# Splitting the first load of A by row tile in a three-term float32 matrix kernel

## The reference

```python
base = x @ W.T                                   # W: 1024 x 1024
gates1 = top-2 softmax of (x @ Wr.T + 5 * one_hot(language))      # 8 experts
c = base + 2 * sum over experts of gates1[e] * (x @ A[e].T) @ B[e].T   # rank 16
y = c @ Wf.T + bf
gates2 = softmax(c @ Wrf.T)                      # 4 experts
y = y + 2 * sum over experts of gates2[e] * (c @ Af[e].T) @ Bm[e].T    # rank 8
out = x + y
```

## Time and profile before

| | |
|---|---|
| device time, median of 3 runs | 324.57 us (324.01 to 324.74) |
| the profiled execution's own time | 324.45 us |
| its span in the trace | 323.1 us |
| PE busy | 319.5 us, 99% |
| DVE busy | 245.1 us, 76% |
| ACT busy | 127.9 us, 40% |
| HBM read and written | 18.97 MB and 8.39 MB |

### The profile page before, as it was taken

One profiled execution on the slowest core, in us unless ns is written; L12 is line 12 of the kernel. 1 busy time (PEld: TensorE's weight loads), 2 busy tenths in 40 slices (PEclk: granted clock), 3 DMA queues, 4 the chain that ended last, 5 costly groups with the idle time before them and its releaser, 6 DMA issues.

```text
span 323.1 us, 5951 instructions
## 1 busy us (share of the span) xinstructions
PE 319.5 (99%) x2255; PEld 313.4 (97%) x2255; DVE 245.1 (76%) x540; ACT 127.9 (40%) x253; POOL 1.4 (0%) x11
## 2 busy tenths in 40 slices
PE   8999999999999999999999999999999999999996
PEld 5999999999999899899999999999999999999996
DVE  3999999998799778988866856757585595665543
ACT  3882846495147236225413503411430340342111
POOL 1000000000000000000000000000000000000000
PEclk9999999999999999999999999999999999999999
DMA  7999000000000311700330250060042015003003
GB/s 261 416 408 284 9 2 0 2 0 2 0 2 0 132 30 40 262 0 0 115 149 0 73 187 0 14 245 0 0 144 116 0 65 195 0 0 130 0 0 130
DMA packets 10702, 27.55 MB, mean 85 GB/s; under 512 B 3166, under 2 KB 4702, under 8 KB 10688
## 3 DMA queue, kind: packets, MB, share of 16 engines
q1 hardware_dynamic: 10256, 26.83, 23.5%
q10 hardware_dynamic: 432, 0.53, 0.5%
HBM read 18.97 MB, written 8.39 MB: 85 GB/s over the span
## 4 chain that ended last, share of the span: by engine, by line
PE 98%; DMA 1%; DVE 0%; issue 0%
PE sums L1269 97%; DMA in<-part 1%; PE sums L1508 1%; DVE rows L1047 0%; DVE b_high L775 0%
## 5 line engine op out<-in xcount | busy, mean ns | idle before, releaser
L1269 PE MATMUL sums<-b_high,a_high 128*128 128x256 f32 (+1 forms) x224 | 45.9, 289 | 0.2 <-DVE b_high L775 0.2
L1269 PE MATMUL sums<-b_low,a_high 128*128 128x256 f32 (+1 forms) x224 | 45.5, 287 | 0.0
L1269 PE MATMUL sums<-b_high,a_low 128*128 128x256 f32 (+1 forms) x224 | 45.5, 286 | 0.0
L1269 PEld LDWEIGHTS sums<-b_high,a_high 128*128 128x128 f32 x224 | 35.2, 191 | 1.1 <-ACT a_high L527 1.1
L1269 PEld LDWEIGHTS sums<-b_low,a_high 128*128 128x128 f32 x224 | 35.1, 191 | 0.0
L1269 PEld LDWEIGHTS sums<-b_high,a_low 128*128 128x128 f32 x224 | 34.9, 190 | 0.0
L1047 DVE TENSOR_TENSOR rows<-sums,rows 128x354 f32<-128x354 f32 x48 | 24.4, 522 | 9.7 <-PE sums L1269 9.3
L1047 DVE TENSOR_TENSOR narrow<-sums,narrow 128x244 f32<-128x244 f32 x30 | 12.4, 412 | 25.6 <-PE sums L1269 25.6
L1269 PE MATMUL sums<-t_high,s_high 128*128 128x354 f32 x96 | 31.6, 329 | 0.0
L1269 PE MATMUL sums<-t_low,s_high 128*128 128x354 f32 x96 | 31.1, 324 | 0.0
L1269 PE MATMUL sums<-t_high,s_low 128*128 128x354 f32 x96 | 31.1, 324 | 0.0
(11 more groups left out here) (149 smaller groups left out, 821.9 us busy)
## 6 DMA issues: line engine op xcount, KB each, us to landing
stage<-tokens SPq DMA_DIRECT2D x14, 512.0 KB, 4.1
out<-rows SPq DMA_DIRECT2D x14, 512.0 KB, 4.8
in<-part SPq DMA_DIRECT2D x7, 585.0 KB, 9.0
in<-part SPq DMA_DIRECT2D x4, 777.0 KB, 14.1
in<-part SPq DMA_DIRECT2D x4, 265.0 KB, 16.6
rows<-tokens SPq DMA_DIRECT2D x2, 512.0 KB, 14.1
out<-rows SPq DMA_DIRECT2D x3, 192.0 KB, 2.3
c_plain<-gate_proj SPq DMA_DIRECT2D x1, 544.0 KB, 18.3
```

What stands on the lines that cost most here:

```text
L1269: return nc.tensor.matmul(out_, lhs, rhs, start=start, stop=stop, skip_group_check=True)
```

## The change

A's columns for row tiles 0 and 1 come in two transfers of 128 columns instead of one of 256. ACT rounds each in an instruction of its own, DVE subtracts each in an instruction of its own, and PE's first six matmuls stand in another order. The number and the shapes of the matmuls are as before. One transfer is added on SP's queue ahead of everything else that SP issues.

```diff
-        here_2_first = [sem(f"here_2_first_{i}") for i in range(3)]
+        here_2_first = [sem(f"here_2_first_{i}") for i in range(4)]
...
-            sp.dma_start(in_2[:, 0, 2 * P:ROWS_A], part_2[0, :, 2 * P:ROWS_A]).then_inc(here_2_first[0], 16)
+            sp.dma_start(in_2[:, 0, row_tile(0)], part_2[0, :, row_tile(0)]).then_inc(here_2_first[0], 16)
+            sp.dma_start(in_2[:, 0, row_tile(1)], part_2[0, :, row_tile(1)]).then_inc(here_2_first[3], 16)
             sp.dma_start(in_2[:, 0, 0:2 * P], part_2[0, :, 0:2 * P]).then_inc(here_2[0], 16)
...
             act.wait_ge(here_2_first[0], 16)
-            copy(a_high[:, 0, 2 * P:ROWS_A], a12[:, 0, 2 * P:ROWS_A]).then_inc(first_high, 1)
+            copy(a_high[:, 0, row_tile(0)], a12[:, 0, row_tile(0)]).then_inc(first_high, 1)
+            act.wait_ge(here_2_first[3], 16)
+            copy(a_high[:, 0, row_tile(1)], a12[:, 0, row_tile(1)]).then_inc(first_high, 1)
...
             dve.wait_ge(first_high, 1)
-            low_part(a_low[:, 0, 2 * P:ROWS_A], a12[:, 0, 2 * P:ROWS_A], a_high[:, 0, 2 * P:ROWS_A])\
-                .then_inc(first_low, 1)
+            low_part(a_low[:, 0, row_tile(0)], a12[:, 0, row_tile(0)], a_high[:, 0, row_tile(0)]).then_inc(first_low, 1)
             dve.wait_ge(first_b_high, 1)
             low_part(b_low[:, 0, 0:CUT[1]], b21[:, 0, 0:CUT[1]], b_high[:, 0, 0:CUT[1]]).then_inc(first_low, 1)
             dve.wait_ge(first_high, 2)
+            low_part(a_low[:, 0, row_tile(1)], a12[:, 0, row_tile(1)], a_high[:, 0, row_tile(1)]).then_inc(first_low, 1)
+            dve.wait_ge(first_high, 3)
             low_part(a_low[:, 0, 0:2 * P], a12[:, 0, 0:2 * P], a_high[:, 0, 0:2 * P]).then_inc(first_low, 1)
...
             pe.wait_ge(first_high, 1)
             pe.wait_ge(first_b_high, 1)
-            for dt in range(2):
-                rows_product(0, dt, 0, HH)
+            rows_product(0, 0, 0, HH)
             pe.wait_ge(first_low, 1)
-            for dt in range(2):
-                rows_product(0, dt, 0, LH)
+            rows_product(0, 0, 0, LH)
+            pe.wait_ge(first_high, 2)
+            rows_product(0, 1, 0, HH)
             pe.wait_ge(first_low, 2)
             for dt in range(2):
                 rows_product(0, dt, 0, HL)
             pe.wait_ge(first_low, 3)
+            rows_product(0, 1, 0, LH)
+            pe.wait_ge(first_low, 4)
             tiles_product(0, 1, 0)
```

More of the change, by code:

```diff
@@ L781, in vector_program @@
             dve.wait_ge(first_high, 2)
+            low_part(a_low[:, 0, row_tile(1)], a12[:, 0, row_tile(1)], a_high[:, 0, row_tile(1)]).then_inc(first_low, 1)
+            dve.wait_ge(first_high, 3)
             low_part(a_low[:, 0, 0:2 * P], a12[:, 0, 0:2 * P], a_high[:, 0, 0:2 * P]).then_inc(first_low, 1)
-            dve.wait_ge(first_high, 3)
+            dve.wait_ge(first_high, 4)
             low_part(b_low[:, 0, CUT[1]:HB], b21[:, 0, CUT[1]:HB], b_high[:, 0, CUT[1]:HB]).then_inc(first_low, 1)
-            dve.wait_ge(first_high, 4)
+            dve.wait_ge(first_high, 5)
             low_part(bt_low[:, HALF, :], low_rank_in[Q_P2][:, 0, :], bt_high[:, HALF, :]).then_inc(op_split, 1)
@@ L1322, in tensor_program @@
             pe.wait_ge(first_low, 3)
+            rows_product(0, 1, 0, LH)
+            pe.wait_ge(first_low, 4)
             tiles_product(0, 1, 0)
-            pe.wait_ge(first_low, 4)
+            pe.wait_ge(first_low, 5)
             tiles_product(0, 0, 1)
```

## The result

| | before | changed |
|---|---|---|
| median of 14 runs each | 324.53 us | 326.29 us |
| lowest to highest | 323.94 to 325.02 | 325.40 to 328.77 |
| ratio to before, with its 95% interval | | 1.0065 (1.0051 to 1.0078) |
| profiled execution, own time and span | 324.45, 323.1 us | 325.93, 323.9 us |

The changed kernel is 0.65% slower by the ratio of the runs (its median lies 1.76 us above), where I had forecast no change. Its times also scatter over 3.4 us instead of 1.1. The spans alone, which each run lists too, have a median of 324.3 us; of 113 runs of the kernel before whose span is listed it is 323.0 to 323.2, by group of runs.

The account below looks back on a forecast made before the run. It took PE, busy 99% of the span, to bound the kernel. To the profiled 324.45 us it added +0.06 for the low part and 0 for all else, making 324.51, stated as 324.5; range 324.0 to 325.1.

Parts of the forecast that it names:

- SP's queue moved back by one issue: Later transfers on SP's queue are issued 0.46 us later; landing was taken to follow bytes in front, so 0.
- my two ends: Prices for tiles 2 and 3: 0 if landing follows bytes in front, 0.34 us lost if it follows the issue.
- B's landing: B's first piece, on the other queue, lands as before: 0, at best 0.17 us earlier.
- B lands earlier: Rival at the first pieces: B gains up to 0.17 us from A's halved piece, giving 324.41 us; chance 0.14.
- The low part in second place: PE's second matmul waits for tile 0's low part from DVE: 0.10 us lost, +0.06 in the sum.
- The room of 0.04 us at chunk 1: At step 1's weights, PE has 0.04 us to spare after chunk 1's rounding, which caps gains from step 0.
- The argument that no gain could pass: PE waits for chunk 1 whatever step 0 gains; over 0.04 us passes only if chunk 1 lands earlier.
- my sign for the queue rival: Chunk 1's rounding at 8.2 us or later would show that SP's queue is late.
- the queue rival: Chunk 1 on SP's queue lands one issue (0.46 us) later, costs 0.42 us, giving 324.87 us; chance 0.15.
- The rival of the late clock: PE's pace rises only behind step 0, whose rest runs at 1.2 GHz: +2.17 us, 326.6 us; chance 0.08.

Follow-up runs that it names:

- e12: Changed kernel, but SP issues chunk 1 and what follows only once tiles 2 and 3 have landed: 325.09 us, ratio 1.0017.
- e13: Changed kernel, but SP issues chunk 1 and what follows only once tile 0 has landed: 324.61 us, ratio 1.0012.
- e15: Changed kernel, but chunk 2 and what follows wait until tiles 2 and 3 have landed; chunk 1 goes ahead: 326.93 us, ratio 1.0080.
- e6: Kernel before, with the 8 KB language table third on SP's queue, behind tiles 2 and 3: 324.53 us, ratio 1.0007.
- e8: Changed kernel with tile 1 moved behind tiles 2 and 3 in every program: 324.85 us, ratio 1.0020.
- e3: Kernel before, with A's first piece split by partitions into two 64 KB transfers with 1 KB rows, one rounding: 327.93 us, ratio 1.0105.
- e2: Changed kernel with one transfer of 256 columns as before; only the roundings, subtractions and PE's order are changed: 324.97 us, ratio 1.0012.
- after_again: Changed kernel run once more on the same chip for a second profile: 326.64 us, ratio 1.0072.
- e9: Changed kernel with four 512-column matmuls on constants between PE's sixth and seventh product: 325.64 us, ratio 1.0046.
- e14: Kernel before, but SP issues chunk 1 and what follows only once A's first piece has landed: 324.21 us, ratio 0.9993.
- e18: Kernel before, again with chunk 1 and what follows held until A's first piece has landed, as in e14: 324.50 us, ratio 0.9998.
- e4: Kernel before, with the 8 KB language table loaded as SP's second transfer: 326.14 us, ratio 1.0048.
- e5: Changed kernel, with tile 1's transfer issued third on ACT's queue instead of by SP: 329.61 us, ratio 1.0163.
- e16: Kernel before, but chunk 2 and what follows wait until tiles 2 and 3 have landed: 324.36 us, ratio 1.0005.
- e1: Kernel before with only A's first transfer split in two; ACT waits for both and rounds 256 columns at once: 327.04 us, ratio 1.0076.

## Why the prediction was wrong

**SP's queue moved back by one issue: I took 0, bounded by 0.34 for tiles 2 and 3. This step failed.** They were rounded 1.29 us later (4.28 to 5.57), almost three times the 0.46 of the issue, and PE's weights loaded at 6.49 instead of 5.37, so 1.12 us late and not 0.34. I read the busy DMA engines as proof that landing follows the bytes in front. The windows say how much moves, not whose packets move: with a large transfer issued 0.48 us behind it, the small one waited. Neither of my two ends knew that case. What was behind the transfer counted, and I only looked in front of it (e12, e13, e15); the place in the queue counted with it (e6, e8).

**B's landing: I took 0, with 0.17 as the good end.** It came 0.39 us earlier, and so it did in every profile in which A's first piece had 128 columns (3.31 to 3.42; 3.62 to 3.73 where it was 128 KB). It is the rival "B lands earlier", with more than twice the 0.17 that I allowed it, and PE did start at 3.77. The Trainium skill, "DMA: Bandwidth & Descriptors", section "Queues, rings and completion order", has the engines take turns between queues packet by packet, and B's sign agrees with it. That A's rows had become shorter isn't needed for it: in e3, with 64 KB in rows of 1 KB, B was rounded at 3.01. The same section says that on one queue each engine consumes in ring order; the landing of tiles 2 and 3 depended all the same on what was issued behind them.

**The low part in second place: I took 0.10.** The second matmul followed the first by 0.35 us as before (3.77 to 4.12; 4.16 to 4.51). It cost nothing. I let the subtraction start at 3.99 because it had started there before; but that start had waited for A's rounding (3.96). Now it began at 3.54, 0.21 behind the start of B's rounding.

**The room of 0.04 us at chunk 1: read from one execution, and not a property of the kernel.** With the very transfers of the kernel before, chunk 1 was rounded at 6.94 in e2. The argument that no gain could pass was weaker than it looked. Chunk 1's rounding at 8.35 met my sign for the queue rival with its price of 0.42. But the loss didn't come by that way: the rounding ended at 8.99, and step 1's weights loaded only at 9.44. It came through tiles 2 and 3.

**The rival of the late clock: 0.08, with +2.17 as its price.** Half of the runs were late. The price in after_again was 1.3 us beside 1.0 of waiting; the 2.17 was for a rise behind the whole of step 0, and it came at 9.5, inside it. I judged it by a pause of 0.10 us; the pause was 1.2. Given the first failure it was as likely as not. A fall of the clock after its rise, to which five of the ten late runs point, had no term of mine. The Trainium skill, "TensorE: Matmul & The Clock Gate", section "What's actually happening", says that the window runs free of the kernel's start; two groups of spans, and e9 without the late one, agree with a rise that a pause can miss or not, depending on its phase. No run here shows the window itself.

**Around the span.** The first group of the changed kernel has a median of 1.7 us outside the span, with half of the runs over 1.8, against 1.3 before. That is the 0.4 us or so that the span doesn't explain. In after_again it is 1.37. In e2 it is 2.0, in e14 1.28 and in e18, the same kernel, 1.43 with four runs over 1.9. I can't tie it to the edit; it stays open.

## What to carry to other kernels

Before adding a small transfer ahead of others, look at what is issued behind it: here the third small one, with a large one issued 0.48 us behind it, came more than a microsecond later, while the DMA engines read busy. Holding the large ones until the first small piece had landed cost nothing (e13, e14, e18); holding them until the last had landed cost 0.8 us of span (e12). A pause of PE of 0.7 to 1.3 us in the first ten cost twice here, once as a wait and in half of the runs again through the clock, so the second piece mattered more than the first.

## What I had not expected of the hardware

- An 8 KB transfer in second place made the next one 0.78 us later (e4), and a transfer in third place on ACT's queue landed 6.7 us after its issue (e5, 1.69 to 8.41).
- Chunk 1's landing hardly depends on its issue: issued at 1.67, 2.15, 3.17, 3.46 and 4.37, it was rounded at 7.83 (6.94 in e2, 7.07 in e16), 8.35 (7.54 in e15), 7.92, 7.42 and 8.26. Why the second place of the kernel before escapes the delay with chunk 1 issued just as close behind stays open.
- After a long pause of PE the granted clock, once up, fell to 0.50 for some 3 us (e3), and the mean clock of half of the late runs of the changed kernel points to the same.
- Two waits in front of ACT's first activation moved its table load of 1.28 us behind the transfer (e1).
